# An edge-attention layer on a graph: SyncE fetches the key and value rows of two of the 196 edge groups

## The chip, the cores and the metric

The kernel runs on one core of a Trainium2 chip. The metric is the device time of one execution in microseconds (us). Its engines are TensorE (PE; its weight loads are listed as PEld), VectorE (DVE), ScalarE (ACT), GpSimd (POOL) and SyncE (SP). SyncE computes nothing here: it waits and issues DMAs. An engine name with a q behind it (SPq, POOLq) is the engine's own instruction queue in the trace, where DMA issues, register loads and moves are seen.

## The reference, cut to what matters

```python
Q_h = (x @ Wq + bq).reshape(N, H, D)             # N = 6250 nodes, H = 8 heads, D = 12
K_h = (x @ Wk + bk).reshape(N, H, D)
V_h = (x @ Wv + bv).reshape(N, H, D)
E = (edge_attr @ We + be).reshape(-1, H, D)      # 100000 edges, sorted by dst
score = K_h[src_idx] * Q_h[dst_idx] / sqrt(D) * E
score = exp(clip(score.sum(-1, keepdims=True), -5.0, 5.0))
wV = segment_sum(V_h[src_idx] * score, dst_idx, num_segments=N)
Z = segment_sum(score, dst_idx, num_segments=N)
x = layernorm(x + (wV / (Z + 1e-06)).reshape(N, H * D))
```

`src` is random; `dst` is sorted, so the edges of a group point to few neighbouring nodes, while their source rows lie all over the table.

## The kernel before, in words

**Tables first.** PE multiplies the transposed x with the weights of keys, values and queries, ACT copies the products (L525) and SyncE stores them in DRAM: `kv_table` (a row of 192 floats, 768 bytes, per node: 96 of the key, 96 of the value) and `q_table` (96 floats per node). `all_tables_stored` is the wait for both.

**Edge groups.** The 100000 edges are cut into 196 groups of 512 edges, each of 4 tiles of 128 edges; the last has 2 tiles. The main loop (the functions called `windowed`, one per engine) runs over the groups, software-pipelined. Four groups are a quad (49 quads).

- GpSimd (L472, called at L484 to L490) fetches a group's rows of keys and values: one indirect DMA per tile, each of 128 rows, with the row numbers in `src_idx`. The destination `kv` is a ring of `KV_RING` = 16 groups. Before it fills a slot again GpSimd waits for `e_msg`, which VectorE raises when it has used the slot's values (L751). The first 9 groups (`EARLY`) come another way: GpSimd gathers rows of x for them before the tables are there, and PE makes keys and values out of them.
- SyncE (L425 to L445) loads for each group the edge features (`load_features`, L393, 192 KB), the edges' node numbers relative to the group's window (`load_rows`, L397, 80 KB), and the window of 80 rows of queries (`load_window`, L401, 30 KB). All three have rings of 8 groups: SyncE waits until ACT has read the old node numbers (`e_dist`) and PE the old features and window (`e_q`). The first 8 groups' features and node numbers are issued before the loop. The window's address comes from a register: once per quad `bases_of` (L339, L340) reads four numbers from `base_i` into SyncE's registers. After every quad SyncE may store finished results (L418).
- ACT turns the node numbers into a one-hot pick of queries (L557, L560), copies E (L566) and takes the exponentials (L571, L572).
- PE multiplies features by weights (L950), picks queries (L957), turns the product of both (L968) and sums messages by node of the window (L981).
- VectorE multiplies E and queries (L720), two iterations later by the keys (L730, `times_keys`, which waits for `e_kv`: the group's rows have landed), sums heads (L737), one iteration later builds the pick (L712), weighs the values (L751, `weigh_v`, raises `e_msg`), and adds the window's sums to the accumulator (L766).

So a group's `weigh_v` stands in VectorE's order behind the `queries_times_features` (L720) of the group three further on.

What fixes the order of SyncE's work is the program text: the loop over quads, and within it rows, features and window of one group after another, each behind its wait. Nothing is planned at run time but the path (L335, L337), one register that every engine loads before the loop.

Of the kernel before, what the change touches and what calls it, by code (L numbers as in the profile page):

```python
# [39 lines left out]
P = 128  # L40
# [12 lines left out]
QUAD = 4  # L53
# [19 lines left out]
FIRST_TILES = [*range(0, NODE_TILES - LAST_TILES, FINAL_TILES), NODE_TILES - LAST_TILES, NODE_TILES]  # L73
STEPS = len(FIRST_TILES) - 1
FINAL_RING = 3
KV_RING, EA_RING, REL_RING, QWIN_RING, PICK_RING, MSG_RING = 16, 8, 8, 8, 4, 4
QE_RING = 3

GENERAL, WINDOWED, STREAMED = 0, 1, 2
IN_RANGE = "the least of node numbers below N_NODES, and of N_NODES where edges are padded"  # L80


# [11 lines left out]

def edges_in(tile):
    return min(P, N_EDGES - tile * P)


def steps_at(group, lag, streamed):
# [26 lines left out]
    return sum(len(stores_of(s)) for s in range(step % FINAL_RING, step, FINAL_RING))  # L126


def build(nc, xT, x_rows, src_cols, dst_cols, dst_rows, eaT, weights, biases, ones, out):
# [5 lines left out]
    assert EA_RING == REL_RING == QWIN_RING and WINDOW <= P  # L135
    assert PICK_RING > ADDED - WEIGHED and MSG_RING >= ADDED - TURNED and QE_RING > TURNED
    assert SUMS * FINAL_TILES + WINDOW <= 512 and LAG_TRANSPOSE == SUMMED + 2
    assert EARLY < KV_RING and tiles_of(EARLY) == GROUP_TILES


# [6 lines left out]
    with ExitStack() as ctx:  # L147
# [55 lines left out]
        room_min = sb("room_min", [1, 1], F32)  # L203
        fits = sb("fits", [1, 1], F32)
        streams = sb("streams", [1, 1], F32)
        base_i = sb("base_i", [1, GROUPS], I32)
        path_i = sb("path_i", [1, 1], I32)


        kv = sb("kv", [P, KV_RING, GROUP_TILES, 2 * DIM], F32)  # L210
        ea = sb("ea", [P, EA_RING, GROUP], F32)
        rel_bc = sb("rel_bc", [WINDOW, REL_RING, GROUP], BF16)
        q_win = sb("q_win", [P, QWIN_RING, DIM], F32)
# [43 lines left out]
        l_src_early = sem("l_src_early")  # L257
        l_src = sem("l_src")
        l_rows = sem("l_rows")
        l_dst = sem("l_dst")  # L260
        l_xn = sem("l_xn")
        c_xones = sem("c_xones")
# [22 lines left out]
        r_cols = sem("r_cols")  # L285
        r_ready = sem("r_ready")
        e_kv = [sem(f"e_kv{i}") for i in range(KV_RING)]
        e_ea = [sem(f"e_ea{i}") for i in range(EA_RING)]
        e_rel = [sem(f"e_rel{i}") for i in range(REL_RING)]
        e_qwin = [sem(f"e_qwin{i}") for i in range(QWIN_RING)]  # L290
# [47 lines left out]

        def bases_of(engine, quad):  # L339
            return nc.values_load_multi_w_load_instructions(  # L340
                base_i[0:1, quad * QUAD:(quad + 1) * QUAD], engines=[engine], min_val=0, max_val=N_NODES,
                skip_runtime_bounds_check_because=IN_RANGE)[1]

        def all_tables_stored(eng):
            for i in range(2):
# [17 lines left out]
        def _(sp):  # L363
# [36 lines left out]
            def load_window(group, base):  # L400
                sp.dma_start(q_win[0:WINDOW, group % QWIN_RING, :], q_table[bass.ds(base, WINDOW), :]  # L401
                             ).then_inc(e_qwin[group % QWIN_RING], 16)

            sp.wait_ge(r_rel, 16)
            for group in range(EA_RING):
                load_features(group)
# [14 lines left out]
            def all_stored():  # L421
                for slot in range(FINAL_RING):
                    sp.wait_ge(f_out[slot], 16 * sum(len(stores_of(s)) for s in range(slot, STEPS, FINAL_RING)))

            def windowed(streamed):  # L425
                all_tables_stored(sp)
                stored = 0
                sp.wait_ge(c_zero, 3)
                for quad in range(QUADS):
                    for group, base in enumerate(bases_of(mybir.EngineType.SP, quad), quad * QUAD):  # L430
                        if group >= EA_RING:
                            sp.wait_ge(e_dist, group - REL_RING + 1)
                            load_rows(group)
                            sp.wait_ge(e_q, group - EA_RING + 1)
                            load_features(group)
                        load_window(group, base)

# [22 lines left out]
        @block.gpsimd  # L460
        def _(pool):
            nc.gpsimd.memset(ident[:], 0.0).then_inc(c_id0, 1)
            pool.wait_ge(c_id0, 1)
            nc.gpsimd.affine_select(out=ident[:], in_=ident[:], compare_op=ALU.not_equal, fill=1.0, base=0,
                                    pattern=[[-1, P]], channel_multiplier=1).then_inc(c_ident, 1)
            nc.gpsimd.iota(iota_i[:], pattern=[[1, SPAN]], base=0, channel_multiplier=0).then_inc(c_iota, 1)
            nc.gpsimd.iota(part_i[:], pattern=[[1, 1]], base=0, channel_multiplier=1).then_inc(c_iota, 1)

            def gather(rows, table, group, t, semaphore):
                tile = group * GROUP_TILES + t  # L470
                n = edges_in(tile)
# [12 lines left out]
            def windowed(streamed):  # L484
                for group in range(EARLY, GROUPS):
                    slot = group % KV_RING
                    if group >= KV_RING:
                        pool.wait_ge(e_msg, group - KV_RING + 1)
                    for t in range(tiles_of(group)):
                        gather(kv[:, slot, t, :], kv_table, group, t, e_kv[slot])  # L490

            def general():
                pool.wait_ge(l_dst, 16)
                pool.wait_ge(x_kv, 2 * EARLY)
                with pool.Fori(0, GROUPS) as group:
# [13 lines left out]

            by_path(pool, path, windowed, general)  # L510
# [3 lines left out]
        def _(act):  # L514
            act.dma_start(rows_i[:], dst_rows).then_inc(l_rows, 16)
            act.dma_start(x_t[DIM:DIM + 1, :], ones[0:1, :]).then_inc(c_xones, 16)
            act.dma_start(dst_idx[:], dst_cols).then_inc(l_dst, 16)
            act.dma_start(early_t[DIM:DIM + 1, :, :], ones[0:1, 0:2 * GROUP]).then_inc(c_ones, 16)
            nc.scalar.preload_act_table_set("natural_log_exp_and_others")
            for pair in range(TABLE_TILES // 2):  # L520
# [113 lines left out]
        def _(dve):  # L634
# [25 lines left out]
            nc.vector.memset(acc_t[:], 0.0).then_inc(c_acc, 1)  # L660

            dve.wait_ge(r_load, 32)
            nc.vector.tensor_copy(base_i[:], base_all[0:1, :]).then_inc(r_cols, 1)
            nc.vector.tensor_reduce(span_max[:], span_row[:], axis=AX_X, op=ALU.max).then_inc(r_cols, 1)
            for step in range(STREAMED_STEPS):
                nc.vector.tensor_reduce(least_after[:, step:step + 1], base_all[0:1, FINISHED_AFTER[step] + 1:GROUPS],
# [54 lines left out]
                                        ps_eq[(2 * group + 1) % 3][0:DIM, 0:n], ALU.mult).then_inc(e_qe, 1)  # L721

            def times_keys(group):
                n, slot = tiles_of(group), group % KV_RING
# [22 lines left out]
            def weigh_v(group):  # L747
# [2 lines left out]
                m = msg[:, group % MSG_RING, 0:n, :]  # L750
                nc.vector.tensor_tensor(  # L751
                    m[:, :, 0:DIM].rearrange("p t (h d) -> p t h d", h=HEADS),
                    kv[:, group % KV_RING, 0:n, DIM:2 * DIM].rearrange("p t (h d) -> p t h d", h=HEADS),
                    weight[:, 0:n, :].unsqueeze(3).to_broadcast([P, n, HEADS, HEAD_DIM]), ALU.mult
                ).then_inc(e_msg, 1)

# [275 lines left out]
            by_path(pe, path, windowed, general)  # L1032


# [39 lines left out]
```

## Time and profile before

| | us |
|---|---|
| median of 3 runs | 1004.61 (1003.4 to 1005.5) |
| the profiled execution, time | 1004.89 |
| the profiled execution, span of the trace | 1003.1 |
| mean granted TensorE clock | 0.874 of full |
| busy: PE / DVE / ACT / POOL | 754.7 / 595.4 / 453.4 / 742.9 |

The time of an execution is 1.8 us more than its span. Busy time leaves out DMA issues, register loads and semaphore waits of SyncE, so SyncE has no line of its own among the busy engines; its work is read from the order of time of its queue.

### The profile page before, as it was taken

The numbers are of one execution on the slowest core, as the hardware profiler recorded it, in microseconds if no ns is written. First come the engines' busy times: TensorE is split into PE (matmuls) and PEld (weight loads), VectorE is DVE, ScalarE is ACT, GpSimd is POOL, SyncE is SP. The second block draws the span as 40 slices with busy tenths as digits, with TensorE's granted clock in tenths as the row PEclk, the third lists the DMA queues.
The fourth block names the chain that finished last, engine by engine and source line by source line (L and its number), as shares of the span: only waits on it lengthen the run. The fifth ranks groups of instructions, "written<-read, shape, count | busy, mean of one in ns | idle before, by whom it ended". The sixth has DMA issues, their size and how long they took to land.

```text
span 1003.1 us, 13052 instructions
## 1 busy us (share of the span) xinstructions
PE 754.7 (75%) x3387; PEld 418.3 (42%) x3387; DVE 595.4 (59%) x1584; ACT 453.4 (45%) x1096; POOL 742.9 (74%) x790
## 2 busy tenths in 40 slices
PE   5899987877777777777876686777768778777763
PEld 4656643433443334343433343434435334343332
DVE  4459965555555655565556556565565656565664
ACT  3477754444444444444435345334444444444421
POOL 6777777777777777777777777777777777777772
PEclk9999998789789898979788989888887987889885
DMA  8997775555555555555554655555545555555321
GB/s 222 310 238 194 203 190 156 155 152 155 147 150 144 141 155 132 143 137 161 133 148 134 157 141 133 158 133 147 151 129 151 149 150 141 140 141 158 99 80 45
DMA packets 124294, 153.03 MB, mean 153 GB/s; under 512 B 57725, under 2 KB 91967, under 8 KB 124212
## 3 DMA queue, kind: packets, MB, share of 16 engines
q0 software_dynamic: 36944, 75.08, 29.7%
q1 hardware_dynamic: 80448, 73.74, 25.8%
q10 hardware_dynamic: 6822, 3.31, 1.3%
q8 instruction: 30, 0.49, 0.2%
q14 instruction: 50, 0.41, 0.1%
HBM read 142.06 MB, written 9.98 MB: 152 GB/s over the span
## 4 chain that ended last, share of the span: by engine, by line
POOL 64%; issue 21%; PE 5%; DMA 4%; DVE 3%; SPq 1%; ACT 0%; POOLq 0%; DVEq 0%
POOL kv L472 64%; DMA kv<-kv_table,src_idx 2%; DMA q_table<-node_stage 1%; DMA w_all<-biases_in 1%; PE ps_eq L902 1%; PE ps_eq L957 1%; SPq L393 1%; PE ps_qe_seg L902 1%; PE ps_eq L950 1%; DMA q_win<-q_table 1%; PE ps_last L902 0%; DVE node_stage L712 0%; SPq L397 0%; DVE ps_last L737 0%; PE ps_eq_qe L902 0%
## 5 line engine op out<-in xcount | busy, mean ns | idle before, releaser
L472 POOL DMA_INDIRECT kv<-kv_table,src_idx x746 | 706.2, 947 | 227.6 <-issue 225.4
L571 ACT ACTIVATE ps_last<-clipped 128x32 f32<-128x32 f32 x196 | 39.4, 201 | 489.2 <-DVE clipped L744 484.6
L957 PE MATMUL ps_eq<-pick_t,q_win 128*96 128x512 f32 (+1 forms) x262 | 156.3, 682 | 18.8 <-ACT e_t L566 17.5
L950 PE MATMUL ps_eq<-ea,w_all 128*96 128x512 f32 (+1 forms) x262 | 161.4, 703 | 8.2 <-DVE qe_t L720 6.6
L730 DVE TENSOR_TENSOR kq<-kv,ps_qe_seg 128x384 f32<-128x384 f32 x98 | 53.9, 550 | 180.2 <-DMA kv<-kv_table,src_idx 180.0
L730 DVE TENSOR_TENSOR kq<-kv,ps_eq_qe 128x384 f32<-128x384 f32 x98 | 54.1, 552 | 176.4 <-DMA kv<-kv_table,src_idx 176.4
L981 PE MATMUL ps_qe_seg<-node_stage 128*104 128x80 f32 x784 | 104.1, 284 | 52.4 <-DVE acc_t L766 38.0
L981 PE MATMUL ps_last<-node_stage 128*104 128x80 f32 x780 | 99.9, 277 | 56.9 <-DVE acc_t L766 48.2
L557 ACT ACTIVATE distance<-rel_bc,neg_part 80x512 bf16<-80x512 bf16 x196 | 138.4, 706 | 2.0 <-issue 1.0
L560 ACT ACTIVATE pick_t<-distance 80x512 f32<-80x512 bf16 x196 | 123.2, 629 | 6.2
L981 PEld LDWEIGHTS ps_qe_seg<-node_stage 128*104 128x104 f32 x784 | 94.0, 198 | 60.7 <-DVE node_stage L751 45.0
L981 PEld LDWEIGHTS ps_last<-node_stage 128*104 128x104 f32 x780 | 89.6, 190 | 65.5 <-DVE node_stage L751 56.3
L737 DVE TENSOR_REDUCE ps_last<-kq 128x32 f32<-128x384 f32 x196 | 107.5, 549 | 0.0
L751 DVE TENSOR_TENSOR node_stage<-kv,ps_last 128x384 f32<-128x384 f32 x196 | 106.2, 542 | 0.0
L957 PEld LDWEIGHTS ps_eq<-pick_t,q_win 128*96 128x96 f32 x262 | 44.3, 186 | 121.4 <-issue 119.9
L712 DVE TENSOR_TENSOR node_stage<-ps_last,rel_f 128x320 f32<-128x320 f32 x196 | 94.4, 482 | 0.0
L720 DVE TENSOR_TENSOR qe_t<-e_t,ps_eq 96x512 f32<-96x512 f32 x131 | 88.2, 673 | 7.6 <-ACT e_t L566 7.2
L968 PEld LDWEIGHTS ps_qe_seg<-ident,qe_t 96*128 96x128 f32 x390 | 45.9, 154 | 109.9 <-DVE kq L730 68.2
L968 PEld LDWEIGHTS ps_eq_qe<-ident,qe_t 96*128 96x128 f32 x392 | 44.8, 152 | 109.3 <-DVE kq L730 69.8
L957 PE MATMUL ps_eq_qe<-pick_t,q_win 128*96 128x512 f32 x130 | 79.7, 700 | 6.6 <-ACT e_t L566 6.3
L950 PE MATMUL ps_eq_qe<-ea,w_all 128*96 128x512 f32 x130 | 81.1, 710 | 4.4 <-DVE qe_t L720 4.4
L968 PE MATMUL ps_qe_seg<-ident,qe_t 96*128 96x96 f32 x390 | 55.0, 267 | 34.1 <-DVE kq L730 34.1
(85 smaller groups left out, 663.5 us busy)
## 6 DMA issues: line engine op xcount, KB each, us to landing
ea<-ea_t_in SPq DMA_DIRECT2D x196, 192.0 KB
rel_bc<-rel_rows_dram SPq DMA_DIRECT2D x196, 80.0 KB
kv<-kv_table,src_idx POOLq DMA_INDIRECT x746
q_win<-q_table SPq DMA_DIRECT2D x196, 30.0 KB
kv_table<-node_stage SPq DMA_DIRECT2D x5, 960.0 KB, 6.1
x_both<-x_t_in SPq DMA_DIRECT2D x5, 480.0 KB, 12.4
q_table<-node_stage SPq DMA_DIRECT2D x5, 480.0 KB, 7.6
x_both<-x_rows_in ACTq DMA_DIRECT2D x10, 240.0 KB, 3.5
```

Source lines behind the costliest of these rows:

```text
L472: pool.indirect_dma_start(rows[0:n, :], None, table, bass.IndirectOffsetOnAxis(ap=src_idx[0:n, tile:tile + 1], axis=0)).then_inc(semaphore ...
L557: nc.scalar.activation(distance[:, b, 0:n], rel_bc[:, slot, 0:n], ACT.Abs, bias=neg_part[0:WINDOW, :]).then_inc(e_dist, 1)
L560: nc.scalar.activation(pick_t[0:WINDOW, group % 3, 0:n], distance[:, b, 0:n], ACT.Relu, bias=1.0, scale=-1.0).then_inc(e_pt, 1)
L712: nc.vector.tensor_tensor(pick[:, group % PICK_RING, 0:n, :], window_iota.unsqueeze(1).to_broadcast([P, n, WINDOW]), rel.unsqueeze(2).to_b ...
L720: nc.vector.tensor_tensor(qe_t[:, group % QE_RING, 0:n], e_t[:, group % 2, 0:n], ps_eq[(2 * group + 1) % 3][0:DIM, 0:n], ALU.mult).then_in ...
L730: nc.vector.tensor_tensor(kq[:, group % 2, 0:n, :], kv[:, slot, 0:n, 0:DIM], ps_qe[group % 2][:, 0:n * DIM].rearrange("p (t d) -> p t d", ...
L737: nc.vector.tensor_reduce(score[:, group % 2, 0:n, :], kq[:, group % 2, 0:n, :].rearrange("p t (h d) -> p t h d", h=HEADS), axis=AX_X, op= ...
L751: nc.vector.tensor_tensor(m[:, :, 0:DIM].rearrange("p t (h d) -> p t h d", h=HEADS), kv[:, group % KV_RING, 0:n, DIM:2 * DIM].rearrange("p ...
L950: nc.tensor.matmul(ps_eq[2 * group % 3][0:DIM, 0:n], w_e, ea[:, slot, 0:n], start=True, stop=True).then_inc(e_e, 1)
L957: nc.tensor.matmul(ps_eq[(2 * group + 1) % 3][0:DIM, 0:n], q_win[:, slot, :], pick_t[:, group % 3, 0:n], start=True, stop=True).then_inc(e ...
L968: last = nc.tensor.transpose(ps_qe[group % 2][:, t * DIM:(t + 1) * DIM], qe_t[:, group % QE_RING, t * P:(t + 1) * P], ident[0:DIM, 0:DIM])
L981: last = nc.tensor.matmul(ps_seg[group % 2][0:SUMS, 0:WINDOW], msg[:, group % MSG_RING, t, :], pick[:, group % PICK_RING, t, :], start=(t ...
```

## The change

Two groups, 98 and 190, are taken from GpSimd and given to SyncE. The 1024 rows of keys and values of these two groups are loaded one by one, each by a DMA of its own of 768 bytes from `kv_table` to one partition, with the row number in a register. In each quad SyncE issues 22 of them, spread over the quad's groups (6, 6, 5 and 5 behind the window load of the group), group 98's 512 rows first and then group 190's: the last of group 98 is issued in quad 23 (groups 92 to 95), the last of group 190 in quad 46 (groups 184 to 187). The two groups have slots of their own behind the ring, which goes from 16 to 13 groups. GpSimd passes over the two groups: of its 746 gathers from `kv_table` (187 groups, the last with 2 tiles) 8 go. Instead of four numbers SyncE loads 26 at the start of a quad (four window bases and 22 row numbers) with one call; the row numbers come in over ACT's DMA queue at the start (`numbers`, 49 pieces of 88 bytes), and SyncE waits for them once. VectorE waits for a row group's four tiles on four semaphores.

```diff
-KV_RING, EA_RING, REL_RING, QWIN_RING, PICK_RING, MSG_RING = 16, 8, 8, 8, 4, 4
+KV_RING, EA_RING, REL_RING, QWIN_RING, PICK_RING, MSG_RING = 13, 8, 8, 8, 4, 4
+SYNC_GROUPS, SYNC_ROWS = (98, 190), 22
+ROW_GROUPS = SYNC_GROUPS
+POOL_GROUPS = [group for group in range(GROUPS) if group not in ROW_GROUPS]
...
+def kv_slot(group):
+    return KV_RING + ROW_GROUPS.index(group) if group in ROW_GROUPS else POOL_GROUPS.index(group) % KV_RING
+def rows_in(quad, groups, per_quad):
+    rows = [(group, row) for group in groups for row in range(GROUP)]
+    return rows[quad * per_quad:(quad + 1) * per_quad]
...
-        base_i = sb("base_i", [1, GROUPS], I32)
+        numbers = sb("numbers", [1, QUADS, QUAD + SYNC_ROWS], I32)
-        kv = sb("kv", [P, KV_RING, GROUP_TILES, 2 * DIM], F32)
+        kv = sb("kv", [P, KV_RING + len(ROW_GROUPS), GROUP_TILES, 2 * DIM], F32)
...
+        def load_row(eng, group, row, number):
+            t, p = divmod(row, P)
+            eng.dma_start(kv[p:p + 1, kv_slot(group), t, :], kv_table[bass.ds(number, 1), :]
+                          ).then_inc(e_rows[group][t], 16)
...
+            sp.wait_ge(l_numbers, 16)
             sp.wait_ge(r_rel, 16)
...
                 for quad in range(QUADS):
-                    for group, base in enumerate(bases_of(mybir.EngineType.SP, quad), quad * QUAD):
+                    rows = rows_in(quad, SYNC_GROUPS, SYNC_ROWS)
+                    loaded = numbers_of(quad, QUAD + len(rows))
+                    for i in range(QUAD):
+                        group = quad * QUAD + i
                         if group >= EA_RING:
                             sp.wait_ge(e_dist, group - REL_RING + 1)
                             load_rows(group)
                             sp.wait_ge(e_q, group - EA_RING + 1)
                             load_features(group)
-                        load_window(group, base)
+                        load_window(group, loaded[i])
+                        for (row_group, row), number in [*zip(rows, loaded[QUAD:])][i::QUAD]:
+                            load_row(sp, row_group, row, number)
...
-                for group in range(EARLY, GROUPS):
-                    slot = group % KV_RING
-                    if group >= KV_RING:
-                        pool.wait_ge(e_msg, group - KV_RING + 1)
+                for i, group in enumerate(POOL_GROUPS[EARLY:], EARLY):
+                    if i >= KV_RING:
+                        pool.wait_ge(e_msg, POOL_GROUPS[i - KV_RING] + 1)
                     for t in range(tiles_of(group)):
-                        gather(kv[:, slot, t, :], kv_table, group, t, e_kv[slot])
+                        gather(kv[:, kv_slot(group), t, :], kv_table, group, t, e_kv[kv_slot(group)])
...
             act.dma_start(dst_idx[:], dst_cols).then_inc(l_dst, 16)
+            act.dma_start(numbers[:, :, QUAD:], src_sync).then_inc(l_numbers, 16)
...
-            nc.vector.tensor_copy(base_i[:], base_all[0:1, :]).then_inc(r_cols, 1)
+            nc.vector.tensor_copy(numbers[:, :, 0:QUAD], base_all[0:1, :].rearrange("p (n j) -> p n j", j=QUAD)
+                                  ).then_inc(r_cols, 1)
...
-                fetched = sum(tiles_of(g) for g in range(slot, group + 1, KV_RING))
-                dve.wait_ge(e_kv[slot], 16 * fetched)
+                if group in ROW_GROUPS:
+                    for t in range(n):
+                        dve.wait_ge(e_rows[group][t], 16 * P)
+                else:
+                    dve.wait_ge(e_kv[slot], 16 * kv_fetched(group))
```

`numbers_of` is `bases_of` for SyncE with n numbers in place of four; the host makes `src_sync` out of `src`.

## Rows read from the trace of the kernel before

**Rows 1.** The page's first part: busy time of the engines over the span.

```profile
PE 754.7 (75%) x3387; PEld 418.3 (42%) x3387; DVE 595.4 (59%) x1584; ACT 453.4 (45%) x1096; POOL 742.9 (74%) x790
```

**Rows 2.** The page's fourth part: the chain that ended last, by engine.

```profile
POOL 64%; issue 21%; PE 5%; DMA 4%; DVE 3%; SPq 1%; ACT 0%; POOLq 0%; DVEq 0%
```

**Rows 3.** Groups of instructions by line: GpSimd's gathers.

```profile
L472 POOL DMA_INDIRECT kv<-kv_table,src_idx x746 | 706.2, 947 | 227.6 <-issue 225.4 <-DVE node_stage L751 2.1
```

**Rows 4.** Waits of GpSimd after 51 us (total, times, longest).

```profile
POOL kv L472 <- DVE node_stage L751: 2.1, 7, 0.3
```

**Rows 5.** Waits of VectorE, 128 to 990 us.

```profile
DVE kq L730 <- DMA kv<-kv_table,src_idx: 356.4, 162, 4.5
```

**Rows 6.** GpSimd in order of time: gathers at the loop's start, groups 9 and 13.

```profile
51.85 0.94 POOL L472 DMA_INDIRECT kv<-kv_table,src_idx  x1 [0.52 <-issue]
...
71.86 0.95 POOL L472 DMA_INDIRECT kv<-kv_table,src_idx  x1 [0.30 <-issue]
```

**Rows 7.** SyncE's queue at the loop's start: eight windows back to back, then group 10.

```profile
56.79 4.34 SPq L401 DMA_DIRECT2D q_win<-q_table  x8
...
65.85 0.43 SPq L397 DMA_DIRECT2D rel_bc<-rel_rows_dram  x1
66.47 0.32 SPq L393 DMA_DIRECT2D ea<-ea_t_in  x1
66.97 0.32 SPq L401 DMA_DIRECT2D q_win<-q_table  x1
67.34 0.42 SPq L397 DMA_DIRECT2D rel_bc<-rel_rows_dram  x1
```

**Rows 8.** The same stretch cut at 60.15 us: the windows of groups 6 and 7.

```profile
60.15 0.98 SPq L401 DMA_DIRECT2D q_win<-q_table  x2
```

**Rows 9.** Register loads by tile (ns min/median/max): four numbers, then one number.

```profile
L340 SPq TENSOR_LOAD <-base_i x49: 295/298/321, 56.3 to 911.6; - x49
...
L337 SPq TENSOR_LOAD <-path_i x1: 478/478/478, 55.3 to 55.3; - x1
```

**Rows 10.** Waits of SyncE, 128 to 900 us.

```profile
SPq L393 <- PE ps_eq L957: 250.0, 102, 6.2
SPq L397 <- ACT distance L557: 181.9, 95, 5.2
SPq L393 <- PE ps_eq_qe L957: 124.2, 51, 6.1
```

**Rows 11.** The chain in order of time, at the loop's start and end.

```profile
56.79 5.07 DMA q_win<-q_table
...
984.21 2.34 DMA kv<-kv_table,src_idx
```

**Rows 12.** All engines in order of time: query pick of group 3, then VectorE.

```profile
67.47 1.02 PE L957 MATMUL ps_eq<-pick_t,q_win 128*96 128x512 f32 x2
68.60 0.68 DVE L720 TENSOR_TENSOR qe_t<-e_t,ps_eq 96x512 f32<-96x512 f32 x1
70.53 0.54 DVE L751 TENSOR_TENSOR node_stage<-kv,ps_last 128x384 f32<-128x384 f32 x1
```

**Rows 13.** VectorE in order of time: key products of groups 0, 22 and 23.

```profile
67.23 0.54 DVE L730 TENSOR_TENSOR kq<-kv,ps_eq_qe 128x384 f32<-128x384 f32 x1
...
126.21 0.54 DVE L730 TENSOR_TENSOR kq<-kv,ps_eq_qe 128x384 f32<-128x384 f32 x1
...
130.06 0.55 DVE L730 TENSOR_TENSOR kq<-kv,ps_qe_seg 128x384 f32<-128x384 f32 x1 [0.99 <-DMA kv<-kv_table,src_idx]
```

**Rows 14.** VectorE near the end: key product of group 195.

```profile
986.57 0.35 DVE L730 TENSOR_TENSOR kq<-kv,ps_qe_seg 128x192 f32<-128x192 f32 x1
```

**Rows 15.** Busy time by stretch; the last three columns are PE clock, DMA share, GB/s.

```profile
63.00:128.00 65.00, 65.00 (x353) 37.99 (x352) 61.95 (x157) 52.51 (x120) 49.17 (x52) 1.00 0.77 206
...
520.00:960.00 440.00, 325.61 (x1442) 173.59 (x1440) 260.67 (x718) 195.78 (x488) 333.02 (x352) 0.87 0.53 141
```

**Rows 16.** The page's third part: SyncE's DMA queue (packets, MB, share of 16 engines).

```profile
q1 hardware_dynamic: 80448, 73.74, 25.8%
```

More of the change, by code:

```diff
@@ L75 @@
 FINAL_RING = 3
-KV_RING, EA_RING, REL_RING, QWIN_RING, PICK_RING, MSG_RING = 16, 8, 8, 8, 4, 4
+KV_RING, EA_RING, REL_RING, QWIN_RING, PICK_RING, MSG_RING = 13, 8, 8, 8, 4, 4
 QE_RING = 3
+SYNC_GROUPS, SYNC_ROWS = (98, 190), 22
+ROW_GROUPS = SYNC_GROUPS
+POOL_GROUPS = [group for group in range(GROUPS) if group not in ROW_GROUPS]
 GENERAL, WINDOWED, STREAMED = 0, 1, 2
+IN_TABLES = "node numbers below N_NODES, and N_NODES where edges are padded"
 IN_RANGE = "the least of node numbers below N_NODES, and of N_NODES where edges are padded"
@@ L96, in edges_in, with kv_fetched @@
     return min(P, N_EDGES - tile * P)
+def kv_slot(group):
+    return KV_RING + ROW_GROUPS.index(group) if group in ROW_GROUPS else POOL_GROUPS.index(group) % KV_RING
+def kv_fetched(group):
+    slot, last = kv_slot(group), POOL_GROUPS.index(group)
+    return sum(tiles_of(POOL_GROUPS[i]) for i in range(slot, last + 1, KV_RING))
+def rows_in(quad, groups, per_quad):
+    rows = [(group, row) for group in groups for row in range(GROUP)]
+    return rows[quad * per_quad:(quad + 1) * per_quad]
 def steps_at(group, lag, streamed):
@@ L126, in stores_before, with build @@
     return sum(len(stores_of(s)) for s in range(step % FINAL_RING, step, FINAL_RING))
-def build(nc, xT, x_rows, src_cols, dst_cols, dst_rows, eaT, weights, biases, ones, out):
+def build(nc, xT, x_rows, src_cols, src_sync, dst_cols, dst_rows, eaT, weights, biases, ones, out):
     assert GROUPS % QUAD == 0 and TABLE_TILES % STAGE == 0 and STAGE % 2 == 0
@@ L137, in build @@
     assert SUMS * FINAL_TILES + WINDOW <= 512 and LAG_TRANSPOSE == SUMMED + 2
+    for groups, rows in ((SYNC_GROUPS, SYNC_ROWS),):
+        for i, group in enumerate(groups):
+            assert EARLY <= QUAD * -(-(i + 1) * GROUP // rows) < group < GROUPS - 1
     assert EARLY < KV_RING and tiles_of(EARLY) == GROUP_TILES
@@ L259, in build @@
         l_rows = sem("l_rows")
+        l_numbers = sem("l_numbers")
         l_dst = sem("l_dst")
@@ L287, in build @@
         e_kv = [sem(f"e_kv{i}") for i in range(KV_RING)]
+        e_rows = {group: [sem(f"e_rows{group}_{t}") for t in range(GROUP_TILES)] for group in ROW_GROUPS}
         e_ea = [sem(f"e_ea{i}") for i in range(EA_RING)]
@@ L340, in bases_of @@
             return nc.values_load_multi_w_load_instructions(
-                base_i[0:1, quad * QUAD:(quad + 1) * QUAD], engines=[engine], min_val=0, max_val=N_NODES,
+                numbers[0:1, quad, 0:QUAD], engines=[engine], min_val=0, max_val=N_NODES,
                 skip_runtime_bounds_check_because=IN_RANGE)[1]
+        def load_row(eng, group, row, number):
+            t, p = divmod(row, P)
+            eng.dma_start(kv[p:p + 1, kv_slot(group), t, :], kv_table[bass.ds(number, 1), :]
+                          ).then_inc(e_rows[group][t], 16)
         def all_tables_stored(eng):
@@ L423, in all_stored, with numbers_of @@
                     sp.wait_ge(f_out[slot], 16 * sum(len(stores_of(s)) for s in range(slot, STEPS, FINAL_RING)))
+            def numbers_of(quad, n):
+                return nc.values_load_multi_w_load_instructions(
+                    numbers[0:1, quad, 0:n], engines=[mybir.EngineType.SP], min_val=0, max_val=N_NODES,
+                    skip_runtime_bounds_check_because=IN_TABLES)[1]
             def windowed(streamed):
@@ L723, in times_keys @@
             def times_keys(group):
-                n, slot = tiles_of(group), group % KV_RING
-                fetched = sum(tiles_of(g) for g in range(slot, group + 1, KV_RING))
-                dve.wait_ge(e_kv[slot], 16 * fetched)
+                n, slot = tiles_of(group), kv_slot(group)
+                if group in ROW_GROUPS:
[3 more added lines that the diff above has]
+                    dve.wait_ge(e_kv[slot], 16 * kv_fetched(group))
                 if group < EARLY:
@@ L752, in weigh_v @@
                     m[:, :, 0:DIM].rearrange("p t (h d) -> p t h d", h=HEADS),
-                    kv[:, group % KV_RING, 0:n, DIM:2 * DIM].rearrange("p t (h d) -> p t h d", h=HEADS),
+                    kv[:, kv_slot(group), 0:n, DIM:2 * DIM].rearrange("p t (h d) -> p t h d", h=HEADS),
                     weight[:, 0:n, :].unsqueeze(3).to_broadcast([P, n, HEADS, HEAD_DIM]), ALU.mult
@@ L1032, in _, with rows_of @@
             by_path(pe, path, windowed, general)
+def rows_of(src, groups, per_quad):
+    rows = np.zeros(QUADS * per_quad, np.int32)
+    rows[:len(groups) * GROUP] = src.reshape(GROUPS, GROUP)[list(groups)].reshape(-1)
+    return rows.reshape(1, QUADS, per_quad)
 def kernel(x, src, dst, edge_attr_96, L0_gnn_Wq, L0_gnn_bq, L0_gnn_Wk, L0_gnn_bk, L0_gnn_We, L0_gnn_be,
@@ L1055 @@
         "src_cols_in": np.ascontiguousarray(src_padded.reshape(-1, P).T).view(np.uint32),
+        "src_sync_in": rows_of(src_padded, SYNC_GROUPS, SYNC_ROWS),
         "dst_cols_in": np.ascontiguousarray(dst_padded.reshape(-1, P).T).view(np.uint32),
@@ L1069 @@
     out = nc.dram_tensor("out", [N_NODES, DIM], F32, kind="ExternalOutput").ap()
-    build(nc, ap["x_t_in"], ap["x_rows_in"], ap["src_cols_in"], ap["dst_cols_in"], ap["dst_rows_in"],
+    build(nc, ap["x_t_in"], ap["x_rows_in"], ap["src_cols_in"], ap["src_sync_in"], ap["dst_cols_in"], ap["dst_rows_in"],
           ap["ea_t_in"], ap["weights_in"], ap["biases_in"], ap["ones_in"], out)
```

## The prediction, as it was written before the result

> **What bounds the kernel now.** I read the chain of waits first, then GpSimd alone, then the others' idle time, and then SyncE's queue, because the change moves work from the first to the last.
>
> PE has the most busy time, 754.7 us, and GpSimd 742.9 [rows 1]; but the chain that ended last is GpSimd with 64% and issue with 21% [rows 2], and the issue is GpSimd's own: its 746 gathers take 947 ns each and leave 227.6 us of gaps, of which 225.4 are issue [rows 3]. One gather costs 0.947 + 227.6/746 = 1.252 us, a group of four 5.0 us, and 746 of them 934 us. After 51 us it waits for a free slot 7 times, 0.3 us each, which is the ordinary gap [rows 4]: it never stands still. VectorE waits 356 us for gathered rows [rows 5]. With the rows there it needs less: from the key product of group 0 (67.23) to that of group 22 (126.21) it does 22 groups in 59.0 us, 2.7 us each, on the stock that GpSimd laid in, and only at group 23 does it meet the first wait for rows [rows 13]. So every gather that goes is worth 1.25 us, as long as nothing else needs more than 5.0 us per group.
>
> SyncE now has time to spare: between 128 and 900 us it waits 250.0 + 181.9 + 124.2 = 556 of 772 us for its rings [rows 10].
>
> **What goes.** 8 gathers x 1.252 = 10.0 us of GpSimd. Does it reach the end? At group 98 VectorE has one group of rows in hand and the next arrives 5.0 us earlier; working at 2.7 us it has made up the difference within two groups. Behind group 190 five groups are left, in which it can make up 2.3 us each against 5.0 (one stop for a node step falls in there, some 3 us), so the end too moves by the full 5.0. From GpSimd's end on everything is as before: -10.0.
>
> **What SyncE gets.** 1024 row loads, each of which has the form of the window load: the register arithmetic, a move and a DMA issue with a register address. A window load that follows the feature load starts 0.50 us after it (66.47 to 66.97), and the next issue comes 0.37 after it (67.34) [rows 7], so 0.13 is address and 0.37 issue. Back to back the eight windows take 4.34 us; less one register load of 0.3 and the last one's 0.32, that is 7 intervals of 0.53 [rows 7, 9], the last of them 0.66 (the pair that begins at 60.15 ends at 61.13, so group 7 begins at 60.81) [rows 8]. A row costs 0.50 at the least and 0.66 at the most; I take 0.515, nearer to the steady 0.50 than to the burst, since nothing in the burst but its start among the big loads is special. That its transfer is small gives no discount: a 192 KB and a 30 KB load are both issued in 0.32 us [rows 7].
>
> The register load: four numbers take 298 ns, and one number 478 ns, on SyncE at the loop's door [rows 9]. So the duration doesn't go by the number between one and four. For 26 the ends are 0.3 us (all fixed) and 26/4 x 0.298 = 1.94 (all by number). Nothing decides between them, so I take the middle, 1.1. The Trainium skill ("Runtime: NRT & Kernel Launch", Instruction fetch mechanics) gives register loads about 200 ns per register, from HBM. By that four would be 0.8 us, where the row shows 0.298, so the trace speaks against it for loads from SBUF; were it right for the 22 added ones, a quad would cost 4.4 us more of SyncE, which is the rival below.
>
> A quad without rows takes SyncE 4 x (three issues): 65.85 to 67.34 for group 10, 1.49 us, with two waits that were nearly open [rows 7], and 1.3 if the wait behind 65.85 is left out (0.50 + 0.37 + the 0.43 of the node numbers); I take 1.35, so 5.4 a quad. In sum 5.4 + 22 x 0.515 + 1.1 = 17.8 us per quad, 4.45 per group. GpSimd's pace is 20.0. So SyncE, idle for most of the time before, is used to 89%, and stays under the bound.
>
> **How much SyncE may need.** Its first window is issued at 56.8 before; 0.8 later now, with the longer register load. If it never waited it would issue the window of group 188 at 57.6 + 47 S, S being its quad. After that it has no rows left, and issues two more windows in 2.6 us (VectorE's key product of a group stands two iterations behind its picks); then 4.7 us (landing, pick, products) to the key product of 188, seven groups at 2.8 and 3 for the node step, and from the last key product 1003.1 - 986.57 = 16.5 us to the end [rows 14], in all 57.6 + 47 S + 46.4. GpSimd's chain ends at 995.6 of span, so S may be up to 18.97 us. At 17.8 there are 1.2 us to spare, at 0.53 per row and a load of 1.94 it is 5.4 + 11.7 + 1.9 = 19.0, just at the edge. This is the number that decides the case.
>
> Until it has caught up, SyncE paces the whole: with windows at 4.45 us per group, and VectorE's product at the window of two groups later plus 4.7, that is at 71.2 + 4.45 g against 15.0 + 5.0 g for the arrival of rows (group 23 at 130.06) [rows 13]; they meet near group 100. Up to there VectorE, PE and ACT run behind SyncE and not, as before, 2.7 us per group; that costs nothing, since GpSimd lays in stock meanwhile, provided that its ring has room.
>
> **The ring of 13.** Before, GpSimd's group 16 needs group 0's slot; now group 13 does, whose first gather starts at 71.86 [rows 6]. In the trace before, group 0's values are used up at 70.53 + 0.54 = 71.07 [rows 12]. That product stands behind the product L720 of group 3, and so behind window 3. Before, windows 0 to 7 are issued in one burst by 61.1 [rows 7]. Now 6 + 6 + 5 rows stand before window 3: it is issued at 57.6 + 3.5 + 3.5 + 3.0 = 67.6. The landing takes at most the 5.07 us of window 0, which had the burst of features before it, and at least the 2.34 of the last gather [rows 11]; I take 3.0. From the start of the pick (67.47) to the end of the weighing (71.07) it is 3.6 us [rows 12]. So the slot is free at 67.6 + 3.0 + 3.6 = 74.2 and GpSimd's gather begins at 74.4: it waits 2.5 us, and never gets them back. The ends: 0 (quick landing, short register load) and 6 (landing 5.1, load of 1.94, rows at 0.6). The next groups: window 4 at 57.6 + 13.0 + 1.1 = 71.7, group 1's slot free at 78.3, wanted at 79.4; window 8 at 86.8, group 5 free at 93.4, wanted at 99.4. One stall, at group 13, and no more.
>
> **The small parts.** The DMA engines: a packet of SyncE's queue takes 0.258 x 16 x 1003 / 80448 = 51 ns [rows 16]. Whether a row is one packet and a completion on one engine, or 16 pieces and 16 completions on all, 1024 x 2 x 51 ns = 104 us falls on the engine or on each: 12 points in the 900 us, on a share of 0.53. The sum, 0.65, is below the 0.77 at which GpSimd kept its pace between 63 and 128 us [rows 15]: nothing. The ACT queue's extra DMA falls before the first table copy, where ACT waits for PE: nothing, at most its issue of 0.4. VectorE's three extra semaphore waits at two groups: nothing, they are long open (rows of 98 are issued with groups 92 to 95), at most 0.2.
>
> **The sum.** 1004.9 (the profiled execution) - 10.0 + 2.5 = 997.4. The median of the runs lies 0.3 below the profiled execution, so 997.1.
>
> **The rivals.**
> 1. *No stall at the ring* (chance 0.2): landing in 2.3 us and a short register load give 66.8 + 2.3 + 3.6 = 72.7, so a stall of 1 or none: 1004.6 - 10.0 + 0.5 = 995.1.
> 2. *SyncE becomes the bound* (chance 0.24; slower). Place: the row loads of quads 0 to 46; price: 47 us for each us of S above 18.97. It decides from 0.57 us per row with my register load, or from 0.53 with the dear one. With 0.58 and 1.94, S = 20.1 and the span is 57.6 + 945 + 46.4 = 1049, time 1051; at the worst (0.66 and 1.94) S = 21.9, time 1135. For it: the one interval of 0.66 and the mean of 0.53 in the only burst that the trace has; against it: the 0.50 of group 10, and that the duration of the register load doesn't grow from one to four. By the 200 ns per register of the Trainium skill's page, S would be 5.4 + 11.3 + 5.2 = 21.9 as well, which I give 0.02 of this rival's 0.24, as the row for four speaks against it.
> 3. *The gain is eaten up* (chance 0.10): S near 19.1, or a stall of 5 us and more with a second one behind it (window 4 has 1.1 us to spare): 1003 to 1006.
> 4. *The rows don't shorten GpSimd's work* (chance 0.02): the gap between gathers grows. Then 1004.6.
>
> The forecast itself, 10.0 less one stall of 1 to 5 us, has 0.44.
>
> **How the numbers follow.** Faster by over 0.2% (2 us, about what a measurement can tell here): forecast and rival 1, and a little of rival 3: 0.65. Within 0.2%: rivals 3 and 4, 0.11. Slower: rival 2, 0.24. Range: from 993.5 (no stall, and 1 us of scatter and of small gains) up over the forecast's upper end (1001) and rival 3 (1006) to the weakest of rival 2, S up to 19.3, 1012; what is left out is most of rival 2, a little under 0.2. The forecast's own range, with rival 1, is 993.5 to 1001.
>
> **What would show it.** In the changed profile: 738 gathers at 1.25 us; one wait of GpSimd for L751 of some 2.5 us near 72 us, window 3 issued near 67.6; row loads 0.50 to 0.53 apart; one register load per quad of 0.3 to 1.9 us; SyncE's waits for its rings gone in the first half and back after about group 100; VectorE's waits for gathered rows starting near 510 us instead of 130, and none at groups 98 and 190. I am wrong if SyncE hardly waits anywhere and VectorE and PE wait for windows in the second half (rival 2), if GpSimd waits for slots again and again, or if a gather takes longer than 0.95 us beside the row loads.

## The result, and the profile after

The changed kernel takes 1001.37 us in the median of 10 runs (999.06 to 1003.24), the kernel before 1005.62 in 10 runs beside it (1003.4 to 1006.1). The ratio is 0.9957, with a 95% interval of 0.9949 to 0.9966: 4.3 us faster. The forecast was 7.5 us faster, within a range of 993.5 to 1012.

The page of the changed kernel, beside [rows 1 to 3, 16]: busy time; the chain that ended last, by engine; GpSimd's gathers; SyncE's DMA queue.

```profile
PE 725.2 (73%) x3387; PEld 419.7 (42%) x3387; DVE 595.8 (60%) x1584; ACT 453.4 (45%) x1096; POOL 735.7 (74%) x782
...
q1 hardware_dynamic: 82496, 74.53, 26.8%
...
SPq 51%; DMA 16%; issue 14%; PE 8%; POOL 6%; ACT 4%; DVE 1%; POOLq 0%; DVEq 0%
...
L516 POOL DMA_INDIRECT kv<-kv_table,src_idx x738 | 699.8, 948 | 231.6 <-issue 222.3
```

Eight gathers are gone, and one takes what it took. But the chain is now SyncE's queue for half of the span, where it was GpSimd with issue; only from 899.6 us on does it run through GpSimd's gathers. SyncE's waits between 128 and 900 us, all of them, against 556 us before [rows 10]:

```profile
SPq L430 <- ACT distance L601: 4.2, 16, 0.4
SPq L426 <- PE ps_eq L1005: 1.2, 5, 0.3
SPq L426 <- PE ps_eq_qe L1005: 0.6, 2, 0.4
```

Six microseconds in 772: SyncE hardly rests. What it paces is seen in VectorE's waits (128 to 990 us), where the wait for rows of [rows 5] has given way to waiting for E (the first two rows below). E in turn waits for PE, and PE for the features that SyncE loads (the last row, over the whole span):

```profile
DVE qe_t L765 <- ACT e_t L610: 299.6, 142, 7.6
DVE kq L778 <- DMA kv<-kv_table,src_idx: 12.0, 7, 3.2
...
PE ps_eq L998 <- DMA ea<-ea_t_in: 147.4, 61, 6.8
```

Nevertheless GpSimd still sets the end: 11.7 of VectorE's 12.0 us of waiting for rows lie behind 940 us, where it has caught up with the gathers, and GpSimd itself, once in the loop, stands still at two places only, both before 83 us. Its last gather ends at 981.85 in a span of 999.8, 17.95 us before the end; before it was 985.08 of 1003.1, 18.0 before the end. So the 3.3 us between the two profiled executions are GpSimd's alone, and they can be counted. GpSimd in order of time, at the two places where it stands still (idle time before the gather in brackets):

```profile
74.71 0.94 POOL L516 DMA_INDIRECT kv<-kv_table,src_idx  x1 [2.12 <-DVE node_stage L799]
...
82.25 0.94 POOL L516 DMA_INDIRECT kv<-kv_table,src_idx  x1 [2.83 <-DVE node_stage L799]
```

With the ordinary gap of 0.3 taken off, the slot of group 0 (wanted for group 13) costs 1.8 us and that of group 1 (for group 14) 2.5. The first gather of the loop starts at 52.87 instead of 51.85 [rows 6], 1.0. The rest, 738 gathers in 924.6 us, is 1.253 us each instead of 1.251, 1.4 in all. In sum -10.0 + 1.0 + 1.8 + 2.5 + 1.4 = -3.3. What makes the start later and the gathers dearer is not shown.

The two stalls come from the windows. PE's query picks of groups 3 and 4 stand waiting for them:

```profile
70.76 1.10 PE L1005 MATMUL ps_eq<-pick_t,q_win 128*96 128x512 f32 x2 [1.48 <-DMA q_win<-q_table]
...
77.57 1.76 PE L1005 MATMUL ps_eq<-pick_t,q_win 128*96 128x512 f32 x2 [4.52 <-DMA q_win<-q_table]
```

Why SyncE is so busy is seen in two views of its instructions (ns min/median/max): the row loads by line, and the register load (`TENSOR_LOAD`, which reads the numbers of a quad from SBUF into registers) by tile.

```profile
L374 SPq FUSED_REGOPS  x1024: 37/37/42, 59.0 to 931.8; - x171
L374 SPq MOVE kv<-kv_table x1024: 29/29/29, 59.1 to 931.9; - x171
L374 SPq DMA_DIRECT2D kv<-kv_table x1024: 224/228/294, 59.1 to 932.0; - x171
```

```profile
L460 SPq TENSOR_LOAD <-numbers x49: 322/2505/5913, 56.5 to 939.6; - x49
```

A row is issued in 0.228 us where a window takes 0.322, and two rows lie about 0.41 apart. The register load is 2.5 us in the median and up to 5.9. By stretch it alternates: quads 1, 2 and 3, then 46 (16 numbers), 47 and 48 (4 numbers each):

```profile
L460 SPq TENSOR_LOAD <-numbers x1: 5536/5536/5536, 70.0 to 70.0; - x1
...
L460 SPq TENSOR_LOAD <-numbers x1: 2115/2115/2115, 87.1 to 87.1; - x1
...
L460 SPq TENSOR_LOAD <-numbers x1: 5535/5535/5535, 103.7 to 103.7; - x1
...
L460 SPq TENSOR_LOAD <-numbers x1: 1623/1623/1623, 918.6 to 918.6; - x1
...
L460 SPq TENSOR_LOAD <-numbers x1: 1194/1194/1194, 932.2 to 932.2; - x1
...
L460 SPq TENSOR_LOAD <-numbers x1: 322/322/322, 939.6 to 939.6; - x1
```

Odd quads are slow, even ones quick, down to the last two, where the same four numbers take 1.19 and 0.32 us. SyncE's quads last 17 and 20.4 us in turn. From the start of quad 2 to that of quad 46 they take 18.9 us in the mean (quads 0 and 1, whose features and node numbers were issued before the loop, are shorter), just under the 18.97 that the prediction set as the bound.

### The profile page after: what moved, and what is told of

Read it like the earlier page. It is cut to its first block, busy times and chain, and to the rows that moved or that the text cites. A ratio compares the mean times of both kernels' runs of the same rounds, so it can differ in the third digit from the quotient of the medians.

```text
span 999.8 us, 16120 instructions
## 1 busy us (share of the span) xinstructions
PE 725.2 (73%) x3387; PEld 419.7 (42%) x3387; DVE 595.8 (60%) x1584; ACT 453.4 (45%) x1096; POOL 735.7 (74%) x782
## 3 DMA queue, kind: packets, MB, share of 16 engines
q1 hardware_dynamic: 82496, 74.53, 26.8%
## 4 chain that ended last, share of the span: by engine, by line
SPq 51%; DMA 16%; issue 14%; PE 8%; POOL 6%; ACT 4%; DVE 1%; POOLq 0%; DVEq 0%
SPq L374 20%; SPq L460 15%; DMA rel_bc<-rel_rows_dram 11%; POOL kv L516 6%; SPq L426 6%; SPq L434 5%; SPq L430 4%; ACT distance L601 3%; DMA ea<-ea_t_in 3%; PE ps_eq L998 2%; PE ps_eq L1005 1%; PE ps_eq_qe L1005 1%; DMA q_table<-node_stage 1%; DMA w_all<-biases_in 1%; PE ps_last L1029 1%
## 5 line engine op out<-in xcount | busy, mean ns | idle before, releaser
L601 ACT ACTIVATE distance<-rel_bc,neg_part 80x512 bf16<-80x512 bf16 x196 | 141.0, 719 | 452.3 <-DMA rel_bc<-rel_rows_dram 451.7
L998 PEld LDWEIGHTS ps_eq<-ea,w_all 128*96 128x96 f32 x262 | 37.6, 187 | 161.8 <-DMA ea<-ea_t_in 157.2
L765 DVE TENSOR_TENSOR qe_t<-e_t,ps_eq_qe 96x512 f32<-96x512 f32 x65 | 44.2, 681 | 102.7 <-ACT e_t L610 101.1
L1029 PEld LDWEIGHTS ps_last<-node_stage 128*104 128x104 f32 x780 | 95.4, 201 | 5.8 <-DVE node_stage L799 5.8
L1029 PE MATMUL ps_qe_seg<-node_stage 128*104 128x80 f32 x784 | 89.5, 259 | 3.4 <-DVE node_stage L832 2.8
L1016 PEld LDWEIGHTS ps_eq_qe<-ident,qe_t 96*128 96x128 f32 x392 | 53.5, 167 | 76.5 <-issue 60.6
L1029 PEld LDWEIGHTS ps_qe_seg<-node_stage 128*104 128x104 f32 x784 | 82.4, 177 | 4.2 <-issue 4.2
L610 ACT COPY e_t<-ps_eq 96x512 f32<-96x512 f32 x131 | 73.7, 562 | 6.2 <-PE ps_eq L998 6.0
L1016 PE MATMUL ps_eq_qe<-ident,qe_t 96*128 96x96 f32 x392 | 58.3, 280 | 3.0 <-DVE kq L778 3.0
```

Source lines behind the costliest of these rows:

```text
L601: nc.scalar.activation(distance[:, b, 0:n], rel_bc[:, slot, 0:n], ACT.Abs, bias=neg_part[0:WINDOW, :]).then_inc(e_dist, 1)
L765: nc.vector.tensor_tensor(qe_t[:, group % QE_RING, 0:n], e_t[:, group % 2, 0:n], ps_eq[(2 * group + 1) % 3][0:DIM, 0:n], ALU.mult).then_in ...
L998: nc.tensor.matmul(ps_eq[2 * group % 3][0:DIM, 0:n], w_e, ea[:, slot, 0:n], start=True, stop=True).then_inc(e_e, 1)
L1016: last = nc.tensor.transpose(ps_qe[group % 2][:, t * DIM:(t + 1) * DIM], qe_t[:, group % QE_RING, t * P:(t + 1) * P], ident[0:DIM, 0:DIM])
L1029: last = nc.tensor.matmul(ps_seg[group % 2][0:SUMS, 0:WINDOW], msg[:, group % MSG_RING, t, :], pick[:, group % PICK_RING, t, :], start=(t ...
```

## The experiments

The ratios are each to the kernel before on the same chip. The runs with 28 numbers, with all starts off, with the rows in bulk and with the ring of 13 alone stand beside one set of runs of the kernel before (1004.24, 14 runs), the other four beside another (1004.93, 11 runs).

### Is it the address that makes the register load slow?

The numbers of a quad lie 26 x 4 = 104 bytes apart, so every second quad begins 8 bytes behind a multiple of 16 (here and below counted from the start of the tile `numbers`). The first experiment changes that alone.

```diff
-        numbers = sb("numbers", [1, QUADS, QUAD + SYNC_ROWS], I32)
+        numbers = sb("numbers", [1, QUADS, 28], I32)
```

> The changed kernel, with the numbers of a quad 28 apart in SBUF instead of 26 (112 bytes, a multiple of 16, instead of 104); nothing else. In the changed kernel the register load of a quad takes 2.1 us in even quads and 5.5 in odd ones. Theory A (the address: a load that starts 8 bytes off a multiple of 16 goes number by number): all loads 2.1 us, SyncE's quads 17.0 us each, the second stall of GpSimd (2.5 us at group 14) gone, the first (1.8 us at group 13) left, SyncE waiting for its rings in the second half; time 1001.4 - 2.5 - up to 1.4 = 997.5 to 999. Theory B (something that comes every second quad, such as the fetch of SyncE's instructions): the loads alternate as before and the time stays at 1001.4.

Measured: 996.48 us, ratio 0.9917 (0.9903 to 0.9931), 7.8 us under the kernel before, which ran at 1004.24 beside it. The time lies 1 us under the expected range; the gain lies within it, since 997.5 to 999 was 6.6 to 8.1 us under 1005.6. The register load, SyncE's waits between 128 and 900 us, and GpSimd's gather of group 13:

```profile
L461 SPq TENSOR_LOAD <-numbers x49: 335/2107/2499, 54.2 to 909.8; - x49
```

```profile
SPq L427 <- PE ps_eq L1006: 39.7, 24, 3.6
SPq L427 <- PE ps_eq_qe L1006: 13.6, 11, 4.5
SPq L431 <- ACT distance L602: 2.8, 11, 0.4
```

```profile
75.69 0.94 POOL L517 DMA_INDIRECT kv<-kv_table,src_idx  x1 [4.69 <-DVE node_stage L800]
```

No load is over 2.5 us, SyncE waits again, and a gather with its gap costs 1.250 us. The second stall is gone, as expected, but the first is 4.4 us instead of the 1.8 expected, for a reason that the next section shows; the profiled execution is the slowest of the five. The alternation was the address. The second experiment puts every quad 8 bytes off:

```diff
-                numbers[0:1, quad, 0:n], engines=[mybir.EngineType.SP], ...
+                numbers[0:1, quad, 2:2 + n], engines=[mybir.EngineType.SP], ...
```

(with 28 numbers per quad, and with the two writers of the tile and VectorE's own load of four numbers moved in the same way).

> As the run with 28 numbers per quad, but the numbers of every quad begin 8 bytes behind a multiple of 16. Theory A: every load of 26 takes 5.5 us, a quad of SyncE 20.5 us, above the 18.97 that the prediction worked out as the bound; the end then follows SyncE: 57 + 47 x 20.5 + 46 + 2 = 1069 us, and GpSimd waits for slots again and again. Theory B: no difference to the run with 28 numbers. If SyncE's pace did not matter, the time would stay near 1000.

Measured: 1064.86 us, ratio 1.0612 (1.0591 to 1.0633). The register load, and GpSimd's waits for slots after 51 us:

```profile
L461 SPq TENSOR_LOAD <-numbers x49: 1130/5549/5932, 55.2 to 1013.9; - x49
```

```profile
POOL kv L517 <- DVE node_stage L800: 49.3, 42, 4.8
```

A quad of SyncE takes 20.50 us, and the time follows it, 4 us under what the prediction's formula gives. Between this kernel and the one before it, 8 bytes of address stand for 68 us. The last of this kind takes 27 numbers per quad, 108 bytes, so that the starts go 0, 12, 8, 4 bytes behind a multiple of 16.

```diff
+        numbers = sb("numbers", [1, QUADS, 27], I32)
```

> The changed kernel with the numbers 27 apart (108 bytes), so that the loads begin 0, 12, 8, 4 bytes behind a multiple of 16, quad by quad. If only a start at a multiple of 16 is quick: 2.1, 5.5, 5.5, 5.5 us in turn, the mean quad 19.6, some 1025 us. If a start at a multiple of 8 were enough, the changed kernel itself would contradict it. If the slow ones go by the end of the load or its length, the pattern is another one.

Measured: 1028.36 us, a single run; a quad of SyncE takes 19.7 us in the mean. The loads of quads 0 to 4:

```profile
L461 SPq TENSOR_LOAD <-numbers x1: 1870/1870/1870, 57.7 to 57.7; - x1
...
L461 SPq TENSOR_LOAD <-numbers x1: 5526/5526/5526, 71.2 to 71.2; - x1
...
L461 SPq TENSOR_LOAD <-numbers x1: 5544/5544/5544, 88.2 to 88.2; - x1
...
L461 SPq TENSOR_LOAD <-numbers x1: 5546/5546/5546, 108.3 to 108.3; - x1
...
L461 SPq TENSOR_LOAD <-numbers x1: 2090/2090/2090, 128.7 to 128.7; - x1
```

Only a start at a multiple of 16 bytes is quick. Four and 26 numbers take 0.32 and 2.1 us there, 0.08 for each added one; elsewhere 1.19 and 5.54, 0.20 for each. Between this kernel and the last, the time rises by 36.5 us for 0.79 us per quad, 46 for each, where the prediction's formula has 47. The Trainium skill ("Runtime: NRT & Kernel Launch", Instruction fetch mechanics) gives about 200 ns per register for loads from HBM. For SBUF the runs here show that figure only where the start is off 16 bytes, and 0.08 us where it is not.

### What do the rows cost, and what is the gain without them?

```diff
-                    rows = rows_in(quad, SYNC_GROUPS, SYNC_ROWS)
+                    rows = []
                     loaded = numbers_of(quad, QUAD + len(rows))
+                    if quad in (4, 5):
+                        row_group = SYNC_GROUPS[quad - 4]
+                        for t in range(GROUP_TILES):
+                            sp.dma_start(kv[:, kv_slot(row_group), t, :], kv_table[t * P:(t + 1) * P, :]
+                                         ).then_inc(e_rows[row_group][t], 16)
```

This kernel leaves out the rows that groups 98 and 190 really need, and SyncE loads four numbers per quad.

> The 1024 row loads are left out; SyncE fills the slots of groups 98 and 190 with eight loads of 128 consecutive rows each (so these two groups work on other nodes' rows), and loads four numbers per quad. Ring of 13 and GpSimd's passing over the two groups stay. This is the gain alone. If the 10.0 us are all there and only the rows and the longer register load take from it: no wait of GpSimd at group 13 (windows in one burst again), 1005.6 - 10.0 = 995.6. If the ring of 13 alone costs: a stall near 72 us and 996 to 998. If the last 5 us are lost at group 190: 1000.

Measured: 996.9 us, ratio 0.9923 (0.9909 to 0.9937), the same as with all 1024 rows and quick register loads (0.9917), within what can be told. So 1024 single row loads cost nothing measurable against eight loads in bulk, as long as SyncE stays under its bound. But there was a stall at group 13, although the first eight windows go out in one burst. GpSimd in order of time:

```profile
75.09 0.94 POOL L522 DMA_INDIRECT kv<-kv_table,src_idx  x1 [4.09 <-DVE node_stage L805]
```

The windows are not to blame here. PE has waited before: for rows of x for the last early groups. The same wait in the kernel with 28 numbers, PE in order of time:

```profile
57.54 1.09 PE L963 MATMUL ps_last<-ident,kv 128*96 128x128 f32 x4 [4.02 <-DMA kv<-x_rows_in,src_idx]
58.42 2.77 PE L975 MATMUL ps_eq_qe<-w_all,early_t 97*128 97x192 f32 x8
```

Eight such products take 1.47 us before that, at a granted clock of 1.00 between 46 and 51 us (2.4 GHz). After the idle 4 us they run at a granted clock of 0.50 between 57 and 63 us (1.2 GHz) and take 2.77. So the main loop starts later by the wait and by the slower clock, ACT's first pick at 65.2 instead of 60.7 us. How long this wait is differs from kernel to kernel (none in the kernel before and in the changed one, 3.1 us here, 4.0 with 28 numbers). Nothing was changed in that stage, and why the wait differs is not shown.

### The ring

The kernel before with 13 slots and nothing else:

```diff
-KV_RING, EA_RING, REL_RING, QWIN_RING, PICK_RING, MSG_RING = 16, 8, 8, 8, 4, 4
+KV_RING, EA_RING, REL_RING, QWIN_RING, PICK_RING, MSG_RING = 13, 8, 8, 8, 4, 4
```

> The kernel before with a ring of 13 slots instead of 16 and nothing else. The slot of group 0 is free at 71.07 in the trace before and GpSimd would want it at 71.56. My theory (the ring alone costs nothing, it needs the late windows): no wait over 0.3 us at group 13, time as before, 1005.6 within 0.5. Rival (the ring costs by itself): a wait of 1 us and more, 1006.5 to 1008.

Measured: 1006.67 us over 10 runs (1004.51 to 1010.71), ratio 1.0029 (1.0014 to 1.0043): 1.4 to 4.3 us slower. My theory falls; the ring does cost by itself. In the profiled execution, with all windows in one burst, the gather of group 13 waited 1.24 us:

```profile
73.17 0.94 POOL L472 DMA_INDIRECT kv<-kv_table,src_idx  x1 [1.24 <-DVE node_stage L751]
```

The 71.07 of the trace before was one draw of a time that varies by several microseconds over the traces here. With 16 slots GpSimd wants group 0's at 86.6 and doesn't notice; with 13 it wants it at 71.6. The next kernel builds on the one with 28 numbers and takes the windows' part of the stall away:

```diff
-    return rows[quad * per_quad:(quad + 1) * per_quad]
+    return rows[(quad - 1) * per_quad:quad * per_quad] if quad else []
...
+                        given = [*zip(rows, loaded[QUAD:])]
+                        if quad == 1:
+                            given = given if i == QUAD - 1 else []
+                        else:
+                            given = given[i::QUAD]
```

(with 23 rows per quad).

> The kernel with 28 numbers per quad, and no rows in quad 0, all of quad 1's behind its four windows, 23 rows per quad from quad 1 on: the first eight windows are issued in one burst, as before the change. Theory (late windows and a late early stage both hold up group 0's values, whichever is later): the stall at group 13 is between 0 and 4 us, as the early products come, and never from a window; time 995 to 996.5, at best 1.5 under the kernel with 28 numbers. Rival (the windows set the stall): no stall over 0.5 us, 994.5.

Measured: 996.01 us, ratio 0.9915 (0.9899 to 0.9932). The profiled execution had no stall at all (span 993.9), but two of six runs took 998.6 and more. A stall of up to 4 us, as the theory has it, would explain them, but none of these two was profiled. The median is that of the kernel with 28 numbers within what can be told. Then one more slot on top of this, with one fewer in SyncE's three rings:

```diff
-KV_RING, EA_RING, REL_RING, QWIN_RING, PICK_RING, MSG_RING = 13, 8, 8, 8, 4, 4
+KV_RING, EA_RING, REL_RING, QWIN_RING, PICK_RING, MSG_RING = 14, 7, 7, 7, 4, 4
```

> As the kernel with late rows, with 14 slots in GpSimd's ring instead of 13, and 7 instead of 8 in the rings of features, node numbers and windows (that is where the room comes from). GpSimd wants group 0's slot 5.0 us later. If the stall at group 13 came from the ring's size: it is gone, 0 to 0.3 us, and with it the scatter; time 994 to 995. If the shorter rings of SyncE cost: over 997.

Measured: 995.53 us (994.11 to 996.78, 4 runs), ratio 0.9906 (0.9891 to 0.9921), a little above the 994 to 995 expected. It has the lowest median, but its interval overlaps those of its neighbours, and four runs are too few to tell whether the scatter is smaller. So no gain from the larger ring is shown here. GpSimd's first wait for a slot, for group 14, in its profile:

```profile
76.34 0.94 POOL L522 DMA_INDIRECT kv<-kv_table,src_idx  x1 [0.30 <-DVE node_stage L805]
```

This is the ordinary gap, although PE waited 2.2 us for the rows of x in this execution too and then ran at a granted clock of 0.72 between 57 and 63 us.

### Two more gathers

```diff
-ROW_GROUPS = SYNC_GROUPS
+ROW_GROUPS = (*SYNC_GROUPS, 195)      # 160 rows, in group 98's slot
...
+                            if (row_group, row) == (195, 0):
+                                sp.wait_ge(e_msg, 99)
```

(Built on the kernel with late rows; 25 rows per quad, 32 numbers apart.)

> As the kernel with late rows, but 25 rows per quad (32 numbers apart), and SyncE also loads the 160 rows of the last group, 195, into the slot that group 98 has left: GpSimd has 10 gathers fewer instead of 8. SyncE's quad is 17.0 + 3 x 0.49 = 18.5 us, under the 18.97 of the prediction. If GpSimd's chain still sets the end: 2 x 1.25 = 2.5 us under the kernel with late rows, 993 to 994. Rival (the end is set by what follows the last gathers, or by SyncE): no gain against the kernel with late rows, 995.5 or more.

Measured: 996.41 us (994.47 to 1000.68), ratio 0.9923 (0.9904 to 0.9942): no gain. In the profiled execution the last gather ended at 972.33 of 992.9, 20.6 us before the end, where it was 18.0: the last group is ready, but the one before it and a node step now stand between the last gather and the end. The 2.6 us more are what the two gathers would have given (2.5). SyncE's quads lasted 18.5 us in the mean; behind 900 us VectorE waited for gathered rows (28.0 us) and not for E, so SyncE did not hold up the end.

## Why the prediction was right, and where not

**What bounds the kernel, and the gain**: right. GpSimd's chain set the end before and after, and eight gathers at 1.25 us are gone. With the rows loaded in bulk the median falls by 7.3 us. The profile of that kernel adds up too: its last gather ends 7.6 us earlier than before, which is the 10.0, a start 0.6 and gathers 0.8 earlier in all, less the stall of 3.8.

**The first stall, at group 13**: right in place, mechanism and nearly in size. Window 3 was forecast for 67.6 and came at 67.63, PE's pick waited for it until 70.76 (forecast 70.6), the gather of group 13 was forecast for 74.4 and came at 74.71; it waited less than the 2.5 us forecast, as GpSimd itself was 1.0 late. What the prediction did not see is that a ring of 13 stalls without late windows as well. The step "the slot of group 0 is free at 71.07" took one execution for a fixed time; with all windows in one burst the stall was 0.9 us with the ring of 13 alone and 3.8 with the rows in bulk.

**"One stall, at group 13, and no more"**: wrong. Window 4 was forecast for 71.7 and came at 75.75, since the register load of quad 1 took 5.5 us instead of 1.1. This is the failed term: the range for the load, 0.3 to 1.94 us, was built on "nothing or in proportion to four numbers", and nearly all real loads lay outside it: 2.1 us in the even quads, 5.5 in the odd ones. The rows of before couldn't show it, since 4 numbers are 16 bytes and all its loads began at a multiple of 16. I had laid the Trainium skill's 200 ns per register aside because the row for four spoke against it; it came true in every second quad.

**The row load**: about 0.41 us instead of 0.515. "That its transfer is small gives no discount" was wrong: the issue of a row takes 0.228 us, that of a window 0.322. The queue's packets rose by 82496 - 80448 = 2048, two per row, which fits the first of the prediction's two cases.

**SyncE's quad**: forecast 17.8, measured 18.9 in the mean. 22 x (0.515 - 0.41) = 2.3 us too much for the rows and 3.8 - 1.1 = 2.7 too little for the loads nearly cancel, and the other twelve issues took some 0.6 more, which gives 18.8; now and then an issue or a store of results takes longer. With the even loads in all quads it would have been 17.0; with the odd ones in all it was 20.5, and the time some 63 us more. That two terms were off by more than their ranges and the sum still came to lie just under the bound is luck.

**Where SyncE has time to spare**: wrong. The prediction had SyncE waiting for its rings again, and VectorE waiting for gathered rows, from about group 100 and 510 us on, and named as a sign of being wrong that SyncE hardly waits anywhere while VectorE and PE wait for windows in the second half. That sign came, with features in place of windows: SyncE waits 6 us in 772, and VectorE catches up with the gathers only near 940 us. At 18.9 us a quad is 4.7 us per group instead of 4.45; with that, the prediction's own two lines meet not near group 100 but near the last. What the sign was to stand for, a time set by SyncE (rival 2), did not come, by a narrow margin.

**The bound of 18.97**: borne out in the main. At 18.5 (the kernel with ten gathers fewer) SyncE does not hold up the end. At 20.50 the formula gives 57.6 + 47 x 20.50 + 46.4 + 1.8 = 1069.3, measured 1064.9; at 19.7 the single run took 1028.4. A straight line through these two reaches the changed kernel's 1001.4 at 19.1 us, an estimate. Why the gathers of the changed kernel take 1.4 us more over the whole stays open: with 28 numbers they are back at 1.250, but with SyncE's quads at 19.7 and at 20.5 they take, without the waits over 0.4 us, 1.251, so SyncE's pace alone does not explain it.

Of the forecast's 7.5 us 4.3 came. The profiled execution lies 4.3 us above the 997.4 forecast for it: 2.5 for the second stall, 1.4 for the dearer gathers and 1.0 for the later start, less 0.7 for the shorter first stall. With quick loads the second stall is gone and the gain is 7.8.

## What to carry to other kernels

When work moves to a queue that looks idle, work out its time per round, and put beside it the time per round that the bound leaves it; here a quad of 18.9 us still left a gain of 4.3 us, and one of 19.7 us turned it into a loss of more than 20. Lay data that an engine loads into registers on 16-byte starts: two unused numbers per quad raised the gain from 4.3 to 7.8 us. A ring's size also buys tolerance for a start that varies, and one profiled execution doesn't show by how much.

## What was not expected of the hardware

- A register load from SBUF by SyncE takes 2.1 us for 26 numbers when it starts at a multiple of 16 bytes from the start of the tile, and 5.5 us when it starts 4, 8 or 12 bytes behind one; for 4 numbers 0.32 and 1.19. VectorE's loads of four numbers show it too: 0.34 us with 28 numbers per quad, 0.96 with all starts 8 bytes off.
- A DMA of one row of 768 bytes to one partition is issued in 0.228 us, one of 80 rows in 0.322, both with a register address.
- 2048 more packets, 5 or 6 row loads every 5 us, left the gathers at 0.95 us each.
